# One exponential over two score pairs becomes two of one pair each, counted pair by pair

## The reference

```python
h = _layernorm(x, axis=-1) * (1 + ca) + sa                 # x: (1, 4096, 256)
q = jnp.einsum('bnhd,hed->bnhe', h.reshape(B, N, 16, 16), Wq)
scores = jnp.einsum('bnhe,bmhe->bhnm', q, q) / NORM        # 16 x 4096 x 4096
attn = jax.nn.softmax(scores, axis=-1)
res = jnp.einsum('bhnm,bmhe->bnhe', attn, q)
x = x + ga * (res.reshape(B, N, D) @ Wp.T + bp)
...                                                        # layernorm, silu feed-forward, residual
```

## Time and profile before

| | |
|---|---|
| median of the runs | 2025.59 us (2025.57 to 2025.62) |
| span of the profiled execution | 2023.6 us, 2.0 us less than the median of the runs |
| granted TensorE clock, mean | 0.998 |
| ACT busy | 1938.3 us, 96% of the span |
| PE busy | 1897.8 us, 94% |
| DVE busy | 1193.2 us, 59% |
| exponentials of 128 x 2048 (L799) | 683, 1936 ns each on average |
| exponentials of 128 x 1024 (L804) | 682, 1118 ns each |

### The profile page before, as it was taken

How to read it: one execution, slowest core, us unless ns; L and a number is a source line. 1 busy time by engine, 2 the same in 40 slices (tenths; PEclk the granted TensorE clock), 3 DMA queues, 4 the chain that set the end, 5 groups by cost and what they waited for, 6 DMA issues and landing times.

```text
span 2023.6 us, 43276 instructions
## 1 busy us (share of the span) xinstructions
PE 1897.8 (94%) x18477; PEld 550.9 (27%) x18477; DVE 1193.2 (59%) x1632; ACT 1938.3 (96%) x1491; POOL 1.3 (0%) x6
## 2 busy tenths in 40 slices
PE   6888889999999999999999999999999999999998
PEld 5411112222222222222222222222222222222225
DVE  7446455765576555755557555765557555575545
ACT  3899999999999999999999999999999999999992
POOL 0000000000000000000000000000000000000000
PEclk9999999999999999999999999999999999999999
DMA  5541111121212212111111211111121111111100
GB/s 164 144 136 43 40 51 42 48 56 42 52 42 52 52 44 60 46 43 46 52 52 46 58 42 50 44 52 53 43 62 44 40 51 55 49 35 38 42 12 12
DMA packets 121346, 108.14 MB, mean 53 GB/s; under 512 B 21936, under 2 KB 120112, under 8 KB 120896
## 3 DMA queue, kind: packets, MB, share of 16 engines
q1 hardware_dynamic: 120400, 103.69, 19.2%
q10 hardware_dynamic: 752, 1.67, 0.2%
HBM read 96.49 MB, written 8.65 MB: 52 GB/s over the span
## 4 chain that ended last, share of the span: by engine, by line
ACT 78%; issue 11%; PE 6%; DVE 1%; DVEq 0%
ACT attend_probs L799 42%; ACT attend_probs L804 34%; PE attend_sums L846 2%; ACT attend_half_tanh L793 1%; PE attend_scores L835 1%; PE attend_out L854 1%; PE attend_scores L854 1%; DVE attend_probs L1020 0%; DVE attend_st L1038 0%; DVE attend_x L1014 0%; ACT attend_ffn_in L810 0%; PE attend_scores L860 0%; DVE attend_st L1219 0%; DVE z L1230 0%; DVE attend_rs L155 0%
## 5 line engine op out<-in xcount | busy, mean ns | idle before, releaser
L799 ACT ACTIVATE attend_probs<-attend_scores 128x2048 f32<-128x2048 f32 x683 | 1322.1, 1936 | 3.4 <-PE attend_scores L835 3.2
L1020 DVE COPY attend_probs<-attend_scores 128x1024 f32<-128x1024 f32 x682 | 835.1, 1225 | 701.4 <-PE attend_scores L835 692.8
L846 PE MATMUL attend_sums<-attend_probs,values 128*17 128x512 f32 x8192 | 1006.8, 597 | 0.3
L804 ACT ACTIVATE attend_probs<-attend_probs 128x1024 f32<-128x1024 f32 x682 | 762.6, 1118 | 1.2 <-DVE attend_probs L1020 1.2
L835 PE MATMUL attend_scores<-asks,keys 64*128 64x512 f16 x4096 | 562.0, 380 | 99.9 <-ACT attend_probs L799 73.6
L835 PEld LDWEIGHTS attend_scores<-asks,keys 64*128 64x128 f16 x4096 | 149.6, 94 | 711.7 <-ACT attend_probs L799 588.2
L846 PEld LDWEIGHTS attend_sums<-attend_probs,values 128*17 128x17 f32 x8192 | 174.0, 96 | 510.3 <-issue 459.1
L854 PE MATMUL attend_out<-w,hidden 128*32 128x256 f32 x1920 | 124.2, 379 | 0.0
L854 PE MATMUL attend_out<-attend_ffn_in,w 128*32 128x512 f32 x896 | 116.6, 592 | 0.0
L854 PEld LDWEIGHTS attend_out<-w,hidden 128*32 128x32 f32 x1920 | 62.0, 110 | 86.4 <-issue 64.3
L1109 DVE TENSOR_SCALAR attend_half_in<-attend_out,b_col 128x512 f32<-128x512 f32 x56 | 42.1, 751 | 16.3 <-PE attend_out L854 14.8
(11 more groups left out here) (146 smaller groups left out, 538.2 us busy)
## 6 DMA issues: line engine op xcount, KB each, us to landing
keys<-parts_dram SPq DMA_DIRECT2D x768, 64.0 KB
keys<-parts_dram SPq DMA_DIRECT2D x256, 56.0 KB
asks<-parts_dram SPq DMA_DIRECT2D x192, 64.0 KB
start_x_in<-L_attn_x SPq DMA_DIRECT2D x8, 512.0 KB, 9.6
parts_dram<-start_q_parts SPq DMA_DIRECT2D x16, 256.0 KB, 2.6
attend_x_now<-L_attn_x SPq DMA_DIRECT2D x8, 512.0 KB, 4.3
out<-base SPq DMA_DIRECT2D x16, 256.0 KB, 2.6
asks<-parts_dram SPq DMA_DIRECT2D x64, 56.0 KB
```

Of the source, the lines that this page charges most:

```text
L799: act.activation(place(n, 2), ps_scores[:, 0:4, :], ACT.Exp, scale=scale).then_inc(exps_done, 1)
L804: act.activation(place(n + 2), place(n + 2), ACT.Exp, scale=scale).then_inc(exps_done, 1)
L846: last = pe.matmul(ps_sums[32 * hq:32 * hq + E1, :], values[:, j + STEPS * b, (gg % Q_GROUPS) * Q_HEADS + hq, :], place(gg * PAIRS + Q_HEA ...
L1020: dve.tensor_copy(place(n), ps_scores[:, 4:6, :]).then_inc(copied, 1)
```

## The change

The exponential over places 0 and 1 becomes two, one of place 0 and one of place 1, each 128 x 1024 with a wait of its own for its own pair and its own place in `probs`. Each counts `exps_done` up by one. So `exps_done` now goes up by three in a round, and `exps_with(n)` is n + 1. PE's code is not edited, but through `exps_with` its wait for place 0 now ends with the exponential of place 0, and its wait for place 1 with that of place 1.

```diff
@@ -99,8 +99,7 @@
 
 def exps_with(n):
 
-    at, i = divmod(n, S_RING)
-    return 2 * at + 1 + i // 2
+    return n + 1
 
 
 class Scope:
@@ -794,9 +793,10 @@
 
                 for at in range(ROUNDS):
                     n = S_RING * at
-                    act.wait_ge(scores_ready, n + 2)
-                    place_free(act, n + 1)
-                    act.activation(place(n, 2), ps_scores[:, 0:4, :], ACT.Exp, scale=scale).then_inc(exps_done, 1)
+                    for i in range(2):
+                        act.wait_ge(scores_ready, n + i + 1)
+                        place_free(act, n + i)
+                        act.activation(place(n + i), ps_scores[:, 2 * i:2 * i + 2, :], ACT.Exp, scale=scale).then_inc(exps_done, 1)
                     if at in TANH_IN:
                         tanh(*TANH_IN[at])
                     if at + 1 < ROUNDS:
```

## The result

The changed kernel took 2061.28 us, the median of two runs (2060.83 and 2061.74), against 2025.59: a ratio of 1.0173, with a 95% interval of 1.0144 to 1.0203. Beside four more kernels on one chip it took 2060.61 us, 1.0174 (1.0158 to 1.0191). So it is slower, by 1.7%. The profiled execution has a span of 2059.1 us, 35.5 more than before.

The account below looks back on a forecast made before the run. The prediction took ACT to be the bound, through its fixed cost per instruction. Profiled span 2023.6 + 37.6 for added instructions - 8.0 of waits = 2053.2, plus 2.0 from span to median: 2055 us, range 2046 to 2084.

Parts of the forecast that it names:

- The price, 0.055 us: On ACT, fixed cost of each of 683 added PSUM exponentials: 0.047 plus 0.008 us, 37.6 us in all.
- The waits at nothing: On ACT, the two waits added per round, on `scores_ready` and `steps_done`, were costed at nothing.
- 8.0 us of waits go: On ACT, of 13.9 us above the floors between starts, 8.0 us would go: late scores, first rounds, copies.
- about 6 us: Where PE's scores come 0.05 to 0.15 us late for L799, all 6 us of ACT's loss would go.
- The waits for DVE's copy become shorter: At six places where L804 waits for DVE's copy, 1.3 of 2.3 us would go, PE being ahead.
- PE gets slack and doesn't take over: PE, the next engine, would get 0.3 us of slack a round; its 2.66 us lies under ACT's 2.757.
- the loop I described: PE refilling banks: about 0.70 us from L799's end to its earliest next start, 0.13 us of slack before the change.
- What would show it: Trace signs: L799 records 1.02 to 1.15 us, starts 0.90 to 0.91 apart, rounds 2.75 to 2.76, PE idle above 99.9.
- Rival 1: Each added PSUM exponential on ACT costs L427's 0.070 us: 2065 us, chance 0.22.
- Rival 2: Between a round's two exponentials, each added instruction costs L804's 0.093 us: 2081 us, chance 0.13.
- rival 3: On ACT the two exponentials don't overlap, 0.170 us beyond the columns each: 2134 us, chance 0.05.
- Rival 4: Not slower or a little faster, PE's loop being the true bound in more rounds: 2014 to 2034 us, chance 0.08.

Follow-up runs that it names:

- e1_coarse: The changed kernel's split exponential, but with the waits and single count of the kernel before: 2063.85 us, 1.0191 of the kernel before.
- e4_banks: The changed kernel with each of its two PSUM exponentials split again, giving four of 512 columns a round: 2143.13 us, 1.0580 of the kernel before.
- e5_sbuf_halves: The kernel before with only place 2's exponential, which reads SBUF, split into two of 512 columns: 2083.57 us, 1.0282 of the kernel before.

## Why the prediction was right, and where it was off

The direction, the size and the bound were right: 2061.28 us measured, 2055 forecast, 2046 to 2084 the range. By its steps:

- **ACT is the bound, and what counts is its number of instructions.** Right. e1_coarse shows that the split alone makes all of the cost, e4_banks that it goes on at the same price for two more.
- **The price, 0.055 us.** Mis-sized: 0.061 by the ends. From L799's 0.047 I had the starts nearly right (0.050 more a round). I added half of the 0.01 by which the rounds of the earlier trace rows exceed the floor, taking it as shared by both instructions of a round. It isn't: the ends lag behind the starts by 0.006 to 0.008 a round before, by 0.017 after, and still by 0.007 in e5_sbuf_halves, where an instruction that reads SBUF was added. So all of it belongs to the one from PSUM. The trace of before could have told it, by L799's own end: in the earlier trace rows it lies at 98.22, and that of the L804 ahead at 96.45. That is 1.77 us, 1.768 as the median of the stage, and 0.060 beyond the 1.708 of its columns, where the starts give 0.047. The same distance is 0.914 for 1024 columns in the changed kernel and 0.487 for 512 in e4_banks, 0.060 beyond the columns each. 683 x 0.061 = 41.7 us, not 37.6.
- **The waits at nothing.** Nearly: with one wait and count, or by pairs on one side, the ends are 2.771 apart, with both by pairs 2.773. That is 1.4 us in all, and the two traces of the kernel before, at 2.712 and 2.711, differ by half as much, so I don't insist on it.
- **8.0 us of waits go.** 5.5 did (7.1 above the ends' rate before, 1.6 after, with the mean taken by starts). The term that was too large is the "about 6 us" of late scores: the 33 rounds held 3.6 us by ends, and all of it went. The rest of the 6, and most of what I called scatter, was the 0.010 a round by which ACT's rate by ends lies above the floors, and that isn't a wait. The copies I had at 1.3 (6 x 0.2, which is 1.2), and they gave 1.4. The first three rounds gave 0.1 in one trace and 1.3 in the other, against 0.7. And the reason was only partly the one I gave: 2.3 of the 3.6 and 0.7 of the 1.9 at the copies go in e1_coarse too, where the order is as tight as before, only because ACT's round is longer. The order brings another 2.0, of which either side alone brings the 1.3 of the late rounds, and only PE's side the 0.7 at the copies.
- **The waits for DVE's copy become shorter.** What they cost does, from 1.9 to 0.5 us. As waits they don't: in the round shown above, the copy holds L804's start back by 0.5 us. But there it costs nothing, since it only uses up the lead of the starts. Before, the lead was at most 0.13 us (records of 1.05 to 1.18).
- **PE gets slack and doesn't take over.** It didn't cost time, as e1_coarse against the changed kernel shows. But the slack doesn't stay: the lead of ACT's starts grows in each round by 0.017, until something stops it. In e1_coarse that is the loop I described: in over half of the rounds L799 starts 0.65 us behind PE's first score matmul. In the changed kernel it isn't PE alone, but DVE's copy behind PE's third pair. In the 165 rounds whose L804 has a record within 0.03 us of the longest, it starts 0.03 us behind the end of its copy in the median (207.81 behind 207.78 in the rows above), while L799 starts 0.49 behind PE's first score matmul, where 0.43 is the least that occurs anywhere. That costs nothing, as long as it only stops the lead.
- **What would show it.** The 0.90 from start to start, L804's 0.947, the round of 2.756 by starts and the missing 1.05 came as I had said. Two signs didn't. L799's records are 1531 ns on average, not 1.02 to 1.15 us, since they hold the lead. And PE's idle time ahead of L835 fell from 99.9 to 68.4 us instead of growing, since the wait for place 1 is counted as busy; in e1_coarse, which lacks that wait, it grew to 134.4.

Sum: 41.4 (681 x (2.7727 - 2.712)) less 5.5 is 35.9, against 35.5 in the spans. It closes by its making, since the 5.5 is what the stage's growth leaves of the 41.4; the columns of the table are the check that doesn't hang on it. My two errors, 4 us and 2.5, went the same way, so it wasn't by their cancelling that the forecast came close.

**Rivals.** Rival 1 (0.070) had the wrong reason: the two exponentials start 0.90 apart, not 0.92. Its price was no further off than mine, though (0.009 against 0.006). Rival 2 (0.093) and rival 3 (no overlap) would have started them 0.95 and 1.02 apart and fall with the same rows; the price of rival 2 is the right one for an instruction that reads SBUF, as e5_sbuf_halves shows with 0.091. So L799's lower figure does belong to its source. The two pages of the Trainium skill that I quoted differ here. "Perfetto Trace Analysis", section "Optimizing Scalar/DVE Operations", gives a cost by the source, 51 ns and 93 ns. By the starts these runs agree with it (50 and 93 ns); by the ends it is 91 ns from SBUF, but 61 from PSUM, and the measurement decides. The formula of "ScalarE: Activation LUTs", section "What ACT_TABLE_LOAD costs", has one figure for both sources, and these runs don't bear that out. Rival 4 falls with the sign.

What stays open: why ACT's starts can run ahead of its ends, and by how much they could without the loop. The rows show only that they do, up to 0.7 us in the changed kernel and 0.8 in e4_banks. The other way round, fewer and larger instructions, such as one exponential for place 2 of two rounds, wasn't tried: it would need its pairs to wait a round longer in `probs`, and by estimate PE, which works 2.66 us in a round with two units, would be the next bound.

## What to carry to other kernels

On a saturated engine count instructions before anything else: a split that makes waits finer is paid once for each instruction, here 0.06 us from PSUM and 0.09 from SBUF, where 1024 columns take 0.85, and it can only win back the waits that there are, which the distance from start to start against its floor bounds from above (here 14 us, of which the ends show 7 to be real). Read that distance rather than durations or idle time where records overlap, and the distance from end to end as well: where they differed here, the ends gave the engine's rate.

## What was not expected of the hardware

ACT's records grew in steady work, with nothing changed in the instruction: L804's from 1.06 to 1.76 us within 41 rounds in the changed kernel, and back to 1.28 behind one wait of 0.5 us. Its mean of 1568 ns against 1118 says nothing of its work. And the kernel before, against itself, came out at 0.9997 with an interval of 0.9988 to 1.0006, and its single runs over all comparisons lay between 2022.75 and 2027.11 us: differences of under 2 us can't be told by times here, though two runs may agree within 0.05 us.
